# TensorE instead of VectorE adds the sums of the node that two chunks share

## The reference

```
seg  = dst * R + edge_type
sums = segment_sum(x[src], seg)            # N x R x F
agg  = sums / max(count(seg), 1)
conv = einsum('nri,rio->no', agg, W_rel) + x @ W_root + bias
h    = conv + x @ W_res + b_res
h    = relu((h - mean) * rsqrt(var + eps) * gamma + beta)
out  = layernorm(x + h)
```

## Time and profile before

| | us |
|---|---|
| median of 3 runs | 2467.42 |
| lowest, highest | 2466.01, 2476.47 |
| profiled execution, its own device time | 2460.68 |
| its span, first to last instruction | 2459.0 |
| before the first gather of a chunk by L532 (span time) | 45.3 |
| after the last such gather | 73.6 |
| chunks | 1563, in 49 groups |

### The profile page before, as it was taken

One profiled execution on the slowest core, in us unless ns is written; L12 is line 12 of the kernel. 1 busy time (PEld: TensorE's weight loads), 2 busy tenths in 40 slices (PEclk: granted clock), 3 DMA queues, 4 the chain that ended last, 5 costly groups with the idle time before them and its releaser, 6 DMA issues.

```text
span 2459.0 us, 36813 instructions
## 1 busy us (share of the span) xinstructions
PE 1856.0 (75%) x10368; PEld 1606.9 (65%) x10368; DVE 1649.4 (67%) x3958; ACT 884.4 (36%) x1651; POOL 1484.2 (60%) x1582
## 2 busy tenths in 40 slices
PE   5787776778688767778777778677767777877888
PEld 3566666667677666666666666666656666666677
DVE  7776675677567567668667667567656766765865
ACT  4333333333333333333333333333333333333333
POOL 6666666666666656666665666666656666666650
PEclk8898899899899889888888889889988988988899
DMA  8534433334443333443343344343333334344333
GB/s 272 155 88 91 90 88 88 90 88 90 92 90 89 88 87 87 90 96 83 89 94 84 86 91 89 84 92 86 88 84 90 88 88 90 88 89 90 86 76 106
DMA packets 244745, 233.79 MB, mean 95 GB/s; under 512 B 27097, under 2 KB 239491, under 8 KB 243907
## 3 DMA queue, kind: packets, MB, share of 16 engines
q0 software_dynamic: 223056, 203.79, 37.1%
q1 hardware_dynamic: 21491, 27.60, 3.6%
HBM read 218.48 MB, written 12.80 MB: 94 GB/s over the span
## 4 chain that ended last, share of the span: by engine, by line
PE 52%; DVE 20%; issue 14%; another core or an unknown queue 10%; ACT 2%; DVEq 2%; DMA 0%; ACTq 0%; SPq 0%; POOL 0%; POOLq 0%
PE ps L636 30%; PE tb L660 19%; DVE onehot L1011 9%; DVE agg L1026 5%; ACT agg L763 2%; PE tb L567 2%; DVEq L350 1%; DVE same L950 1%; DVE tmph L1043 1%; DVEq L1026 0%; DVE lst L1219 0%; DMA eth<-in_edge_type_dram 0%; DVE agg L1243 0%; PE tb L617 0%
## 5 line engine op out<-in xcount | busy, mean ns | idle before, releaser
L532 POOL DMA_INDIRECT xg<-xtab,srcT x1545 | 1457.6, 943 | 885.7 <-PE ps L636 478.4
L636 PE MATMUL ps<-onehot,xg 128*128 128x456 f32 x3126 | 1152.8, 465 | 569.8 <-DVE agg L1026 495.8
L1011 DVE TENSOR_SCALAR onehot<-iota,segT,vT 128x456 fp32r<-128x456 f32 x1563 | 1158.3, 744 | 493.3 <-PE ps L636 400.5
L763 ACT ACTIVATE agg<-ps 128x390 f32 (+1 forms) x1563 | 840.7, 538 | 1514.9 <-PE ps L636 1160.6
L660 PEld LDWEIGHTS tb<-agg,wsb 128*128 128x128 f32 x6370 | 1014.0, 203 | 60.5 <-issue 1.5
L636 PEld LDWEIGHTS ps<-onehot,xg 128*128 128x128 f32 x3126 | 570.2, 220 | 717.7 <-issue 695.8
L660 PE MATMUL tb<-agg,wsb 128*128 128x138 f32 x6370 | 1034.5, 294 | 1.4 <-issue 1.4
L1026 DVE SCALAR_TENSOR_TENSOR agg<-ps,agg 128x65 f32 x1514 | 395.3, 261 | 8.4 <-ACT agg L763 8.1
L1043 DVE SCALAR_TENSOR_TENSOR tmph<-iota,lastg,tb 128x138 f32<-128x138 f32 x49 | 17.6, 358 | 213.9 <-remote 147.6
L950 DVE SCALAR_TENSOR_TENSOR same<-ps,rel 128x1088 bf16<-128x1088 f32 (+3 forms) x96 | 146.0, 1521 | 17.0 <-PE tb L567 15.8
L567 PE MATMUL tb<-same,identb 128*128 128x512 bf16 x416 | 113.0, 397 | 5.2 <-DVE same L950 5.1
(11 more groups left out here) (132 smaller groups left out, 329.1 us busy)
## 6 DMA issues: line engine op xcount, KB each, us to landing
xg<-xtab,srcT POOLq DMA_INDIRECT x1545
xtab<-agg SPq DMA_DIRECT2D x4, 1536.0 KB
hinit<-H SPq DMA_DIRECT2D x1, 3125.0 KB
agg<-in_x_dram SPq DMA_DIRECT2D x4, 768.0 KB, 7.0
out_dram<-agg SPq DMA_DIRECT2D x6, 448.0 KB, 3.0
dsth<-in_dst_dram SPq DMA_DIRECT2D x23, 64.0 KB
eth<-in_edge_type_dram SPq DMA_DIRECT2D x23, 64.0 KB
srcr<-in_src_dram SPq DMA_DIRECT2D x12, 64.0 KB
```

Source lines behind the costliest of these rows:

```text
L532: pool.indirect_dma_start(out=xg[c % RING][:], out_offset=None, in_=xtab.bitcast(F32R), in_offset=bass.IndirectOffsetOnAxis(ap=srcT[t % 2] ...
L636: ins = nc.tensor.matmul(ps[c % NRB][:, 0:OW], rows, onehot[o][:], start=(part == 0), stop=(part == 1))
L763: nc.scalar.activation(agg_group(g)[:, :, bass.ds(off, n)], ps[c % NRB][:, 0:n * R].rearrange("f (n r) -> f r n", r=R), ACT.Copy).then_inc ...
L1011: nc.vector.tensor_scalar(onehot[o][:].rearrange("p (a b) -> p a b", a=3), iota3[:, :, 0:IW], segT[t % 2][:, k:k + 1], vT[t % 2][:, k:k + ...
```

## The change

TensorE adds the shared node itself. `aggregate(c)` multiplies only the 390 own columns of chunk c (456 for the last of a group), and then, unless c is the first of its group, adds two matmuls of 66 columns into the same bank: the rows and the `onehot` of chunk c - 1, columns 390 to 455. The bank that ScalarE copies holds the full sum. `add_carry`, its registers, the semaphore `carried` and all waits for it are gone. Since chunk c now reads `xg` and `onehot` of chunk c - 1, these buffers come free one chunk later: GpSimd waits for chunk c - 17 and not c - 18, VectorE for c - 9 and not c - 10. The products of the group before start at i = 2 and not 4. Some of VectorE's side work moves a few chunks (DVE_COLS, DVE_OFFS, `root_add`, the flag's reduction).

```diff
-DVE_COLS = 117
+DVE_COLS = 114
-DVE_OFFS = 126
+DVE_OFFS = 122
@@ gpsimd
-                pool.wait_ge(agg_ps, c - RING + 1)
+                pool.wait_ge(agg_ps, c - RING + 2)
@@ aggregate(c)
                     pe.wait_ge(evac, c - NRB + 1)
-                    pe.wait_ge(carried, carries(c - NRB + 2))
+                w = OW if last_of_group(c) else W6
+                carried = c % GC > 0
                 for part in range(2):
                     rows = rows_in_sbuf(c)[:, part * F:(part + 1) * F]
-                    ins = nc.tensor.matmul(ps[c % NRB][:, 0:OW], rows, onehot[o][:], start=(part == 0), stop=(part == 1))
+                    ins = nc.tensor.matmul(ps[c % NRB][:, 0:w], rows, onehot[o][:, 0:w], start=(part == 0),
+                                           stop=(part == 1 and not carried))
+                if carried:
+                    o = (c - 1) % NOH
+                    for part in range(2):
+                        rows = rows_in_sbuf(c - 1)[:, part * F:(part + 1) * F]
+                        ins = nc.tensor.matmul(ps[c % NRB][:, 0:R + 1], rows, onehot[o][:, W6:W6 + R + 1], start=False,
+                                               stop=(part == 1))
                 ins.then_inc(agg_ps, 1)
@@ transform(p, lo, hi), lo == 0
-                    pe.wait_ge(carried, carries(min((p + 1) * GC, NCH)))
@@ the loop of TensorE
-                if p >= 1 and i >= TFIRST:
-                    n = pair_len(p) - TFIRST
-                    lo, hi = R * (i - TFIRST) // n, R * (i - TFIRST + 1) // n
+                if p >= 1 and i >= 2:
+                    n = pair_len(p) - 2
+                    lo, hi = R * (i - 2) // n, R * (i - 1) // n
@@ one_hot(c)
-                    dve.wait_ge(agg_ps, c - NOH + 1)
+                    dve.wait_ge(agg_ps, c - NOH + 2)
@@ the loop of VectorE
                 one_hot(c)
-                if c >= CARRY_LAG:
-                    add_carry(c - CARRY_LAG)
```

More of the change, by code:

```diff
@@ L31 @@
 CMAX = 12
-TFIRST = 4
-CARRY_LAG = 11
-CREG = 8
 PE_CMP = 70
@@ L105, in last_of_group @@
         return c % GC == GC - 1 or c == NCH - 1
-    def carries(n):
-        return n - ceil_div(n, GC)
     def pair_len(p):
@@ L272, in gnn @@
         evac = sem("evac")
-        carried = sem("carried")
         root_tr = sem("root_tr")
@@ L1009, in one_hot @@
                 if c >= NOH:
-                    dve.wait_ge(agg_ps, c - NOH + 1)
+                    dve.wait_ge(agg_ps, c - NOH + 2)
                 nc.vector.tensor_scalar(onehot[o][:].rearrange("p (a b) -> p a b", a=3), iota3[:, :, 0:IW], segT[t % 2][:, k:k + 1], vT[t % 2][:, k:k + 1],
                                         ALU.is_equal, ALU.mult).then_inc(oh_rdy, 1)
-            offs = [()]
-            def add_carry(c):
-                t, k = c // TC, c % TC
-                if k % CREG == 0:
-                    dve.wait_ge(offs_rdy, t + 1)
-                    offs[0] = registers(offrow[t % 2][0:1, k:k + CREG], ENG.DVE, WIN - 1)
-                if c % GC == 0:
-                    return
-                dve.wait_ge(evac, c + 1)
-                first = agg_group(c // GC)[:, :, bass.ds(offs[0][k % CREG], 1)]
-                over = ps[(c - 1) % NRB][:, W6:W6 + R].rearrange("f (r n) -> f r n", n=1)
-                nc.vector.scalar_tensor_tensor(out=first, in0=over, scalar=1.0, in1=first, op0=ALU.mult,
-                                               op1=ALU.add).then_inc(carried, 1)
             def root_add(b):
@@ L1083, in _ @@
                 one_hot(c)
-                if c >= CARRY_LAG:
-                    add_carry(c - CARRY_LAG)
                 if c + LO_AHEAD < RING:
                     first_rest(c + LO_AHEAD)
-                if 10 <= c < 10 + 4 * (NROOT - UP) and c % 4 == 2:
-                    root_add(UP + (c - 10) // 4)
+                if 6 <= c < 6 + 4 * (NROOT - UP) and c % 4 == 2:
+                    root_add(UP + (c - 6) // 4)
                 if p >= 2 and i == 6:
@@ L1106, in _ @@
                         offsets_of(t + 1)
-                if c == NCH - GC // 2:
+                if c == NCH - GC:
                     dve.wait_ge(offs_rdy, NTL)
@@ L1111, in _ @@
                     nc.vector.tensor_scalar(col(BAD), tcol[:, 10:11], 0.0, None, ALU.is_gt).then_inc(bad_rdy, 1)
-            for c in range(NCH - CARRY_LAG, NCH):
-                add_carry(c)
             dve.wait_ge(bad_ps, 1)
@@ L1134, in general @@
                 dve.wait_ge(evac, NCH)
-                dve.wait_ge(carried, carries(NCH))
                 dve.wait_ge(g_hin, 16)
```

## The result

| | before | after |
|---|---|---|
| median of 4 runs each, same session | 2469.81 us | 2438.01 us |
| lowest and highest | 2466.01, 2476.47 | 2435.47, 2440.98 |
| ratio after/before | | 0.9879, interval 0.9849 to 0.9909 |
| profiled execution | 2460.7 us | 2441.0 us, span 2439.2 |

The change makes the kernel 1.2% faster. The forecast was 4.4%, 2360 us.

A forecast was written before the change was run, and what follows sets the result against it. No engine is full; waits set the end, chiefly TensorE's 495.8 us for VectorE's addition. 2460.7 + 295 (short matmuls) - 191 (borders) - 212 (inside groups) = 2353, plus 7 for the runs' median: 2360 us, range 2190 to 2500.

The forecast's parts named there:

- What bounds the kernel: Whole kernel: no engine is full, waits set the end; TensorE's largest is 495.8 us for VectorE's addition L1026.
- The added matmuls, +295: TensorE, each chunk: two short matmuls add 0.195 us, times 1514 chunks, +295 us (0 to 295), all on the path.
- The named sign, starts 0.11 us apart: TensorE's new line for 66 columns: 3028 matmuls starting 0.11 us apart at full clock; 0.03 to 0.06 would mean overpriced.
- The border, -191: Between groups: three chunks run while TensorE stood, gaining 3.9 us at each of 49 groups, -191 us.
- Inside the groups, -212: Within groups: three quarters of the remaining 282 us of TensorE's waits for L1026 go, -212 us.
- the condition I named: Inside the groups: if the late reports' lateness keeps its length, all 282 us of waits go.
- my sign (copies over 300 us): TensorE's waits for ScalarE's copies: more than 300 us in total would show that late reports get longer.
- Rival (a): TensorE's reports: late ones get longer, a deeper window only lets TensorE stand later; 2572 us, chance 0.19.
- (c): TensorE's clock: stays up with shorter stalls, rising above 0.93; 2198 us, chance 0.18.
- (d): GpSimd: the gathers become the bound, stalls and added loads vanish in its floor; 2044 us, chance 0.05.
- At nothing: Other engines: L1026 leaving VectorE (395.3 us), buffers freed a chunk later, moved side work and unchanged copies cost nothing.

The follow-up runs named there:

- before_no_add: The kernel before without VectorE's addition of the shared node and all waits for it, that sum left out: 2407.84 us against 2468.93, 0.9738.
- after_third: The changed kernel itself, unaltered, run again beside the kernel before in a later session with late reports: 2401.60 us against 2465.13, 0.9733.
- after_no_short: The changed kernel without its two short matmuls a chunk, the shared node's sum left out: 2406.31 us, 0.9730 against the kernel before.
- free_gather_4: The changed kernel with later gathers going into nine buffers TensorE doesn't read, not waiting for TensorE; late reports: 3897.85 us, kernel before 2460.01.
- after_again: The changed kernel itself, unaltered, run again in a session with prompt reports: 2033.81 us against 2038.54 for the kernel before, 0.9977.
- half_rows_again: The changed kernel with gathers of 512 bytes a row instead of 1 KB, late reports: 2405.77 us, 0.9759 against the kernel before.

## Why the prediction was right or wrong

**What bounds the kernel.** I read rightly that no engine is full and that the rows call TensorE's waits for L1026 the largest. The step that failed is the sum, which adds and subtracts TensorE's time as if TensorE's path set the end. It has two terms wrong. The waits at the border and inside the groups were to give back 191 + 212 = 403 us; taken away alone, in `before_no_add`, they gave back 61. The short matmuls, "I put all of it on the path", were to cost 295 us; with them the kernel took 2401.6 or 2438, without them 2406, so they cost nothing or 32 us at most. The errors have opposite signs: the forecast lay 78 us off and not several hundred by luck.

What the runs show in its place: "GpSimd is not the bound, but it is the next floor" left out that its gathers may slow the others. That is where the rest of the time lies. With TensorE's work as it is, the kernel takes 1849 us without gathers, 1850 with plain transfers, 2034 with gathers and prompt reports, and 2402 to 2438 with late ones. There reports come at half the pace of the gathers while these flow, and nearly all others in GpSimd's pauses; GpSimd pauses when reports don't come. The sign was there in the earlier trace rows: GpSimd's idle time of 885.7 us is 1545 x 0.30 = 464 us between gathers and some 422 us of pauses. That this loop sets the end is the reading that fits all runs; what in it holds the reports is not shown.

**The added matmuls, +295.** The size was nearly right, the place wrong. A stretch at full clock in after, with the chunk of 963.51:

```profile
963.51 0.61 PE L630 MATMUL ps<-onehot,xg 128*128 128x390 f32 x2
963.96 0.31 PE L636 MATMUL ps<-onehot,xg 128*128 128x66 f32 x2
964.10 0.72 PE L660 MATMUL tb<-agg,wsb 128*128 128x138 f32 x4
964.57 0.60 PE L630 MATMUL ps<-onehot,xg 128*128 128x390 f32 x2
```

From chunk to chunk 1.06 us, 1.05 forecast, 0.89 before. But the pair takes 0.14, 0.07 each, where I had 0.11 each, and four products behind it take 0.47 instead of 0.38. It looks as if the products wait for the weights for which the short matmuls did not; no run parts this. The named sign, starts 0.11 us apart, failed; the total of +0.16 came out as +0.17, by a split that I had wrong. Over the whole kernel TensorE's busy time grew by 211 us, with the clock at 0.93 instead of 0.89. The Trainium skill's stream figure ("TensorE: Matmul & The Clock Gate", Back-to-back issue gap), some 81 ns a matmul, is nearer than my 0.11 for the pair by itself; for the whole chunk it gives +0.10 us where the trace shows +0.17.

Of this, nothing is seen on the path: with the short matmuls 2401.6 us and 0.9733, without them 2406.3 and 0.9730, both late and each against the kernel before of its session. No session has the two side by side; against the result's own 2438 it would be 32 us. In the prompt condition it is 2033.8 and 2032.4, again in two sessions. I wrote "I put all of it on the path, though some falls into stalls that remain"; nearly all of it fell there. Only without gathers, or with plain transfers, is TensorE the bound.

**The border, -191.** The mechanism is as described and shown above. Over the groups from the third on, from the start of a group's last chunk to that of the fourth chunk of the next it took 8.8 us before and 6.2 after on average: 2.6 us with the longer chunks in it, where 3.9 less four times 0.195 is 3.1. Sized fairly well, and mostly lost again in the other 28 chunks, which went from 39.8 to 41.8 us a group.

**Inside the groups, -212.** This term carries the larger part of the miss in TensorE's own accounts. With 28 x 0.195 = 5.5 us more work and 212/49 = 4.3 us less waiting, these 28 chunks should have taken 1.1 us longer a group; they took 2.0 longer in the result (1.3 in `after_third`). The waits for L1026 vanished, but the lateness did not keep its length, which was the condition I named: in the middle case a chunk's copy began 1.06 us after the start of its last matmul before, and 4.16 after. The wait for copies by name is short (38.2 us). What came instead, 130 us of halts between products, waits for no semaphore at all; I had no term for it, and my sign (copies over 300 us) could not see it.

**Rival (a)** was right in its mechanism, that a deeper window lets TensorE run on and stand later. All late kernels without the addition's wait show it, with medians of 3.5 to 5.0 us against 1.06, and so do the reports that come in GpSimd's pauses. Not "as long as before", though: TensorE's idle time fell by 231 us. Its price was wrong for the same reason as mine: it charged the 295 us to the path. **(c)**: the clock rose to 0.93 as named, and the time did not follow; `after_no_short` has a clock of 0.865 and the same time. **(d)** was given 0.05 and is what happens in the prompt condition: 2044 by its sum, 2034 measured. **At nothing**: TensorE waits for no gather in after. That the shorter lead of GpSimd lengthens its pauses is a rival that I did not price; `before_no_add`, with the longer lead, is no faster (2408 against 2402, in another session), which speaks against it. VectorE's busy time fell by 257 us and not by L1026's 395: the busy times of its groups overlap, and 1649.4 - 395.3 was no sum to make. Nothing rests on it.

The direction was right and its reason half so: VectorE's addition does cost 61 us, as `before_no_add` shows. How it lengthens GpSimd's pauses (413 us against 359) is argued only: before, TensorE stands at each border (5.67 us in the one shown) and sends no report in that time.

**What stays open.** What makes a session late or prompt. By which resource GpSimd's gathers slow TensorE's stream and hold its reports, and whether scattered rows have a part in it. And why the changed kernel took 2438 in the result's session and 2402 in another, four runs each within 0.3%, at the same time of the kernel before; its trace has as many pauses (325 and 332), longer ones.

## What to carry to other kernels

A wait that ends last on the busiest engine is not yet what sets the end. Nor is an engine whose idle and busy time add up to the span in every variant: that holds for any engine with fixed work. What tells is to take one term away by itself and see what the kernel gives back. Where one engine issues under permits from another, its pauses are part of the bound, and work added to an engine that is held anyway may be free. Run the unchanged and the changed kernel in more than one session before a gain of 1 or 2% is explained; one kernel without the suspected partner (here the gathers) tells more than several that shift the waits.

## What the runs showed of the hardware

In a late session TensorE steps once in 2.80 us in `free_gather_4` while GpSimd issues indirect gathers that never wait for it (35 matmuls in 100 us, 748 without gathers), though it needs nothing of them, and the kernel doubles its time from 1997 to 3898 us. Where the gathers do wait for TensorE (after), its stream runs on at 6.1 matmuls a us, with 244 halts that no semaphore explains, and its reports bunch in GpSimd's pauses. Plain transfers of the same bytes from SyncE do not do that (1850 us in both conditions). The Trainium skill ("DMA: Bandwidth & Descriptors", SWDGE vs HWDGE vs iDMA) says that GpSimd builds a gather's descriptors in software, that VectorE can lock it out of the memory that holds them, and that transfers started by SyncE are immune to that. The plain transfers are spared here too, but the harm goes another way: a gather takes 944 ns in the result and 942 in `after_again`, a selection matrix 741 and 743, and it is TensorE that is held. In the 100 us of `free_gather_4` above a gather does take 1.07 us (77.23 us for 72), but VectorE ran only 6 instructions there, so such a lock does not explain it.

In all other traces one of the 1545 gathers of 128 rows occupies GpSimd for 0.94 us with 1 KB rows and with 512 B rows alike (944 ns in `half_rows_again`), and 0.30 us pass before the next if it has its permit. The 18 gathers at the start, into `wsb`, took some 1.26 us each.
